# Issue order at a phase boundary: the last batch's output projection moved up, the last routing group moved back

## The reference, cut to what matters

```python
x = x + _L0_xattn_ref(_layernorm(x), k, side, ctx, ctx, 8)
x = x + _L0_ffn_ref(_layernorm(x), ...)
x = x + _L1_xattn_ref(_layernorm(x), ctx, ...)   # ends with qdq(o) @ qdq(wp).T + bp
x = x + _L1_ffn_ref(_layernorm(x), ...)
# the last one, on flat = its input as (2048, 256):
scores = jnp.sqrt(jax.nn.softplus(flat @ router_w.T))
_, idx = jax.lax.top_k(scores + expert_bias, 4)
out = sum over experts e of p[:, e] * (silu(clip(x@wg)) * clip(x@wu)) @ wd
out = out + _clamped_swiglu(flat, shared_gate_w, shared_up_w, shared_down_w)
```

## Time and profile before

| | |
|---|---|
| median of 3 runs | 667.66 us (667.11 to 670.08) |
| the profiled execution's own time | 667.93 us |
| its span, first to last instruction | 665.7 us |
| PE busy | 585.4 us, 88% of the span |
| DVE busy | 438.9 us, 66% |
| ACT busy | 385.7 us, 58% |
| POOL busy | 374.1 us, 56% |
| mean granted TensorE clock | 0.964 of full |
| PE's share of the chain that ended last | 70% |

### The profile page before, as it was taken

How to read it: one execution, slowest core, us unless ns; L and a number is a source line. 1 busy time by engine, 2 the same in 40 slices (tenths; PEclk the granted TensorE clock), 3 DMA queues, 4 the chain that set the end, 5 groups by cost and what they waited for, 6 DMA issues and landing times.

```text
span 665.7 us, 14801 instructions
## 1 busy us (share of the span) xinstructions
PE 585.4 (88%) x4205; PEld 470.7 (71%) x4205; DVE 438.9 (66%) x1449; ACT 385.7 (58%) x1133; POOL 374.1 (56%) x527
## 2 busy tenths in 40 slices
PE   1588899999998899997999789778689999999995
PEld 0488787787776687786887557556467788788873
DVE  1546666677766877665866657657495778867663
ACT  2002366756677656786656786774444666656660
POOL 6847847548348357389654542735146565555553
PEclk9999999999999999998999979987599999999999
DMA  7999999999999999423234693799644655555797
GB/s 264 277 178 335 335 334 335 333 333 324 314 315 323 314 321 315 121 81 105 81 105 137 202 314 105 218 285 326 193 132 143 185 161 159 151 154 161 242 413 259
DMA packets 130253, 156.23 MB, mean 235 GB/s; under 512 B 15264, under 2 KB 117280, under 8 KB 129792
## 3 DMA queue, kind: packets, MB, share of 16 engines
q1 hardware_dynamic: 112048, 123.70, 62.4%
q0 software_dynamic: 7632, 20.98, 8.3%
q10 hardware_dynamic: 10496, 10.62, 5.0%
HBM read 54.59 MB, written 100.81 MB: 233 GB/s over the span
## 4 chain that ended last, share of the span: by engine, by line
PE 70%; DVE 11%; POOL 6%; ACT 6%; issue 5%; DMA 0%; ACTq 0%; SPq 0%; POOLq 0%; DVEq 0%
PE ps L431 12%; PE pc L694 12%; PE pS L372 6%; PE pS L674 5%; POOL arena L1451 4%; PE ps L476 3%; PE ps L660 3%; PE po L645 3%; PE ps L606 2%; PE ps L503 2%; PE ps L529 2%; PE ps L520 2%; PE ps L537 2%; PE ps L516 2%; DVE work L735 1%
## 5 line engine op out<-in xcount | busy, mean ns | idle before, releaser
L694 PE MATMUL pc<-arena,tk 128*128 128x128 f32 x768 | 108.3, 294 | 13.3 <-POOL arena L1451 7.3
L694 PEld LDWEIGHTS pc<-arena,tk 128*128 128x128 f32 x768 | 96.6, 201 | 25.7 <-issue 13.5
L431 PE MATMUL ps<-arena,work 128*128 x380 | 100.4, 388 | 1.4 <-ACT work L1201 1.4
L1451 POOL TENSOR_TENSOR arena<-arena 128x512 f32<-128x512 f32 x64 | 90.4, 1427 | 19.8 <-ACT arena L1251 19.6
L1465 POOL DMA_INDIRECT expert_rows<-stage,ixl x64 | 63.9, 999 | 38.7 <-DVE ixl L1082 20.7
L1318 ACT ACTIVATE work<-pS,work 128x128 f32<-128x128 f32 x256 | 72.7, 369 | 3.0 <-DVE work L984 2.9
L431 PEld LDWEIGHTS ps<-arena,work 128*128 128x128 f32 x380 | 66.4, 195 | 7.2 <-issue 1.8
L1191 ACT ACTIVATE tk<-work 128x128 f32<-128x128 f32 x95 | 29.4, 310 | 60.4 <-DVE work L766 55.3
L766 DVE TENSOR_SCALAR work<-ps 128x256 f32<-128x256 f32 x95 | 40.1, 422 | 34.8 <-PE ps L431 34.2
L372 PE MATMUL pS<-arena,tk 128*128 x190 | 60.1, 398 | 1.8 <-ACT tk L1196 1.4
L984 DVE TENSOR_REDUCE work<-pS 128x4 f32<-128x512 f32 x64 | 43.9, 686 | 24.4 <-PE pS L674 24.3
(11 more groups left out here) (330 smaller groups left out, 1471.5 us busy)
## 6 DMA issues: line engine op xcount, KB each, us to landing
expert_rows<-stage SPq DMA_DIRECT2D x32, 2080.0 KB, 21.6
arena<-in_w SPq DMA_DIRECT2D x16, 768.0 KB, 7.4
work<-expert_rows SPq DMA_DIRECT2D x87, 128.5 KB, 2.3
stage<-xn_rows SPq DMA_DIRECT2D x64, 130.0 KB, 2.9
xn_rows<-xnD ACTq DMA_DIRECT2D x16, 512.0 KB, 8.1
arena<-y_rows SPq DMA_DIRECT2D x12, 512.0 KB, 12.3
tk<-in_tk SPq DMA_DIRECT2D x1, 2048.0 KB, 9.5
work<-y_rows SPq DMA_DIRECT2D x4, 512.0 KB, 10.0
```

The source lines that it names most:

```text
L431: i = pe.matmul(p[U * k:U * k + U, 0:256], xgT[n % 3][:, 128 * c + U * k:128 * c + U * k + U], arena[:, 256 * c:][:, bass.ds(e, 256)], sta ...
L694: i = pe.matmul(pv, tk[:, h, 128 * d:128 * d + 128], kvv[:, ci, :, :].rearrange("p b (i h j) -> p (b i) h j", i=8, h=8)[:, :, hl, :], star ...
L1451: pool.tensor_tensor(kv[kk % 4][:, c, half, :].rearrange("p (i h j) -> p i h j", h=8, i=8), i0, i1, ALU.mult).then_inc(s_kv, 1)
```

## The change

For the last batch alone `oiP` and `op` are issued on PE at tick 3077 (1157 + 1920) in place of 3086 and 3090. They now stand ahead of both `tabE` transposes and of `gu` of batch 13, and `op` directly behind `oiP`. All other batches stay where they were. The steps of the last routing group come later in every engine's queue: `ra` by 14 ticks, `rd`, `re`, `top`, `mb`, `rk`, `cum` and `list` by 10, which is one step of the tile loop. No instruction is added to the source or taken from it.

```diff
--- before.py
+++ after.py
@@ -53,7 +53,7 @@
 LATER = {("top", 0): 57, ("top", 1): 45, ("mb", 0): 87, ("mb", 1): 51, ("rk", 0): 101, ("rk", 1): 101,
          ("cum", 0): 105, ("cum", 1): 105, ("list", 0): 143, ("list", 1): -72, ("list", 2): -202,
          ("st", 2): -110, ("list", 3): -182, ("st", 3): -149, ("re", 0): 32, ("rd", 0): -32, ("re", 1): 8}
-LAST = {"ra": -3, "rd": 4, "re": 12, "top": 21, "mb": 23, "rk": 41, "cum": 42, "list": 47, "st": 0}
+LAST = {"ra": 11, "rd": 14, "re": 22, "top": 31, "mb": 33, "rk": 51, "cum": 52, "list": 57, "st": 0}
 STRIDE = (18, 24, 15, 8, 15)
 RG = 4
 SD = 32
@@ -70,6 +70,10 @@
 def at(t, first, every, n):
     d = t - first
     return (d // every,) if d >= 0 and d % every == 0 and d // every < n else ()
+
+
+def per_but_last(t, first, last):
+    return [b for b in range(NB) if (first if b < NB - 1 else last) + BASE[b] == t]
 
 
 def per(t, first, n=1):
@@ -558,13 +562,13 @@
                     pe.wait_ge(s_q, b + 1)
                     pe.transpose(p[:, 0:128], q[b % 2][:, 0:128], ident)
                     pe.transpose(p[:, 128:256], q[b % 2][:, 128:256], ident).then_inc(s_qP, 1)
-                for b in per(t, T_PE["oiP"]):
+                for b in per_but_last(t, T_PE["oiP"], 1157):
                     p, free = bk.take(("oi", b), s_oiT, b + 1)
                     pe.wait_ge(*free)
                     pe.wait_ge(s_oi, b + 1)
                     pe.transpose(p[:, 0:128], xi[1][:, 0:128], ident)
                     pe.transpose(p[:, 128:256], xi[1][:, 128:256], ident).then_inc(s_oiP, 1)
-                for b in per(t, T_PE["op"]):
+                for b in per_but_last(t, T_PE["op"], 1157):
                     p, free = bk.take(("op", b), s_wt, b + 1)
                     pe.wait_ge(*free)
                     pe.wait_ge(s_wint, 2)
```

## The result

The changed kernel took **674.15 us** (median of 14 runs, 670.11 to 676.63) against 667.8 us (14 runs, 664.91 to 670.93) for the kernel before. The ratio is 1.0098, with a 95% interval of 1.0077 to 1.0119: slower by about 6.5 us. The forecast was 672.3, in a range of 669.0 to 676.0. The profiled execution took 673.70 us, 5.77 more than the one of before, with a span of 671.5.

The account below looks back on a forecast made before the run. The last 150 us were taken to hang on PE, so delays entering the dense tile loop carry to the end; 2.62 - 1.03 + 3.00 = 4.59 on the 667.66 median gives 672.3, range 669.0 to 676.0.

Parts of the forecast that it names:

- Part one: Early oiP and op ahead of gu: the residual step waits on DVE behind table copies and clamp, 2.62 later.
- the sum: All delays up to tile 4's clamp: 2.62 - 1.03 + 3.00 = 4.59 us later, clock's fall not counted; chance 0.41.
- Part two: Later routing: tile 0's product gains, shift 1.59; then rd and an extra table load make tile 2's clamp 3.61 later.
- Part three: rk behind step 5: rank product at 492.87, DVE waits about 1.3 for it, tile 4's clamp 4.59 later.
- the rival with the clock: PE's clock falls in new idle gaps near 488 to 492, stretching products up to 1.9: 674.0 to 676.2, chance 0.27.
- two further steps: If the clock falls near 488 to 492, two more tile-loop steps become PE's, at about 1 us each.
- The signs: Expected profile: longer DVE waits, line 989 near 472.5, tables ln, tanh, sqrt, tanh, constant 4 to 5 us shift to the end.
- Cover: Last scatter at 519.3, SyncE's load of tile 25 about 523.5, wanted at 524.7 earliest: costed at nothing, uncovered up to 2.

Follow-up runs that it names:

- this half alone: Changed kernel with the last group's routing put back, leaving only the last batch's early transposes and projection: 670.23 us against 666.79, ratio 1.0046.
- the filled kernel: Changed kernel plus five products on TensorE that nobody reads, placed where it was expected to be idle: ratio 1.0067.
- the one with one table load less: Changed kernel with only the last group's square root moved up from 22 to 16, ahead of tile 0's tanh: ratio 1.0026.
- the routing alone: Kernel before with only the last group's routing one tile step later, the projection where it was: ratio 1.0059.
- the last three runs: Changed kernel with square root earlier (1.0026); early projection, old routing, residual step and normalisation moved up (0.9939); the latter plus 12 unread transposes (0.9953).
- the last but one: Early projection with routing as before, VectorE's residual step and ScalarE's normalisation of the last batch moved up: ratio 0.9939 against the kernel before.
- the two last runs: Early projection, old routing, VectorE's residual step and ScalarE's normalisation moved up (0.9939); the same plus 12 unread TensorE transposes (0.9953).

## Why the prediction was right, point by point

- **Part one held.** Residual step 2.62 later in the sum, 2.64 with this half alone; gu took 2.08 at the lower clock, as assumed. The cause is shown by both directions: the half alone costs it, and moving the step on DVE turns it into 0.97 gained at the residual step, of which only 0.16 reached the tile loop.
- **Part two held in its numbers and not in its reason.** Tile 0's product was forecast at 480.95 and came at 480.95; the top-4 at 486.82 and came at 486.81; tile 2's clamp at 489.88 and came at 489.90. But the sentence "one more table load of 1.28, and it stands on the path" is wrong as a cause. The load was on the path and could be taken away without any gain (the top-4 20.16 after the quantiser's operation in place of 20.23), because the sum had not asked what would stand there instead. The times were right all the same, since the sum went through the whole queue step by step.
- **The 2.66 us for a table switch** that the Trainium skill gives, in "ScalarE: Activation LUTs", section "What ACT_TABLE_LOAD costs", are not seen in any trace here: in the changed kernel the square root started 1.29 after its load began at 485.23, as before.
- **Part three held with the clock kept.** The rank product was forecast at 492.87 and came at 494.30. With the clock held the yardstick is 4.46 over before in the filled kernel and 4.40 in the one with one table load less, against 4.59 in the sum.
- **The likeliest case was the sum alone, 672.3; what happened is the rival with the clock**, at the low end of its cost: 6.35 by the medians, where it had 6.3 to 8.5 over the median. By the traces the fall cost 1.5, of the 1.9 that the rival had for the products; its two further steps at about 1 each did not come. The range held the result. The step that failed is the choice between the two: the sum had the clock's fall at nothing, though the prediction itself named idle times of 1.8 and 1.1 us one behind the other, and the trace after has them as 1.57 and 1.04, with the clock's fall between 490 and 491. I gave it 0.27 and took the other. The fall doesn't always follow from such gaps: the routing alone had 1.58 and 1.03, and the kernel with one table load less 2.82 and 1.23, both with the clock at 1.00.
- **The signs.** The steps came as listed, but for the shift: it is 6.0 at tile 8 and 5.8 in the span (671.5 against 665.7), where 4 to 5 was forecast.
- **Cover.** The late load of tile 25 was hidden, though it came at 527.89 and not at 523.5. Its last scatter is 8.5 later, where the sum had 5.9: 6.0 is the shift, and the rest is one more result and one more scatter of about 1.26 each between the result at 518.11 and the last scatter, where the sum had one such step. The load then came 5.99 after that scatter's start in place of 4.18, and why was not traced.
- **Left open.** On the chip of the last three runs all three kernels come out faster by their ratio than by their traces: 1.0026 where +4.4 us would be 1.006, 0.9939 where -0.85 at tile 4 would be 0.999, and 0.9953 where tile 4's clamp is 0.12 later than before. They have the early projection in common. Earlier loads are not the reason: in every traced kernel with the early projection SyncE's first load of rows starts later after the quantiser's operation than before (4.41 us in the changed kernel, 5.87 in the last but one, 3.55 before). There is no trace of the kernel before on that chip, and this was not tried.

## What to carry to other kernels

When a step is issued earlier on one engine, go through the other engines' queues for it: whatever stands ahead of its consumers there, and is fed by what the step has overtaken, becomes the new wait. Here that was so on VectorE, where the residual step came 2.64 later in place of 0.88 earlier. With that mended it was so again for all that reads the tables: a register load on the very engine of the edit, and ScalarE's normalisation beside it, so that 0.16 of 0.97 us was left, and moving the normalisation alone did not bring the transposes forward (7.07 against 7.08). A register load doesn't count as busy time and is easily overlooked. Moving it as well was not tried. And when a run gives the forecast number, look in its trace whether the step that you moved gave it: the 0.85 came from the clock. Work that is charged to the path should be charged with what would stand there without it; and where a sum opens several idle gaps on TensorE close together, a case with the lower clock belongs among the likely ones and not only in the range.

## What the runs showed of the hardware

Idle gaps alone did not tell whether TensorE's clock falls. Around 1.58 and 1.03 us idle it stayed at 1.00 in one kernel, and around 1.57 and 1.04 it fell to 0.50 in another, where it had come back up 2.2 us later (at 483.9 against 481.7). With 1.57 and 0.76 it fell, on a third kernel, and with 2.82 and 1.23 it stayed up in a fourth. The fall cost 1.5 us.

TensorE's load of table words into registers took 1.25 us in each of the ten traces (1246 to 1257 ns); in the three in which it was the last thing ahead of the last batch's transposes, the next TensorE work started about 0.3 after it ended.

On the chip of the last three runs the kernel before took 689.64 us, against 666.79 and 667.68 on two others, some 3% more, and the traces of the two last runs there have short pauses on DVE and PE that no wait explains. A ratio has to be taken on one chip.
